# Row maxima inside the score contraction, narrower masks, the residual added on VectorE, and a leaner Q/K scratch

## The reference

```python
x = x + attn(layernorm(x), Wq, Wk, Wv, Wo)            # 16 heads of 16, 128 tokens
x = x + ssm(ctx, ctx, layernorm(x), ssm_kernel, D, 8) # 16 heads of 8, long convolution
x = x + ffn(layernorm(x), packed 4-bit weights, scales)

# attn: masked scores are ZERO, not minus infinity, before the softmax
scores = einsum('bthd,bshd->bhts', q, k) * tril(ones)
out = einsum('bhts,bshd->bthd', softmax(scores / 128 ** 0.5), v) @ Wo
# ssm: kv = k_i * v_j over time; y = causal convolution of kv with the head's kernel; out = (y + kv * D) . q
# ffn: (gelu_tanh(x Wg^T) * (x Wu^T)) Wd^T, MLP width 2048, each weight = 4-bit code * scale per block of 32
```

## Time and profile before

| | us |
|---|---|
| median of 3 runs (281.93 to 284.20) | 283.21 |
| profiled execution | 285.32 |
| its span in the profile | 283.6 |
| PE, DVE, ACT, POOL busy | 258.4, 160.6, 123.2, 157.2 |
| mean granted clock of TensorE | 0.973 |

### The profile page before, as it was taken

One profiled execution on the slowest core, in us unless ns is written; L12 is line 12 of the kernel. 1 busy time (PEld: TensorE's weight loads), 2 busy tenths in 40 slices (PEclk: granted clock), 3 DMA queues, 4 the chain that ended last, 5 costly groups with the idle time before them and its releaser, 6 DMA issues.

```text
span 283.6 us, 5339 instructions
## 1 busy us (share of the span) xinstructions
PE 258.4 (91%) x2056; PEld 167.5 (59%) x2056; DVE 160.6 (57%) x264; ACT 123.2 (43%) x257; POOL 157.2 (55%) x193
## 2 busy tenths in 40 slices
PE   0699999997999999996969999999999999999993
PEld 0355766555777777664634566666555666556662
DVE  2879633367775987897576584252635436131124
ACT  2354676553654545644426455323534253442240
POOL 3277264250514788799989897336445563723330
PEclk9999999997999999999579999999999999999998
DMA  6986969707120000003000200000303000000004
GB/s 208 380 296 198 225 203 225 160 4 218 37 82 0 2 2 2 1 3 111 2 0 1 83 30 0 2 0 0 113 0 103 11 0 2 1 0 2 0 0 149
DMA packets 16185, 20.27 MB, mean 71 GB/s; under 512 B 1056, under 2 KB 13856, under 8 KB 16160
## 3 DMA queue, kind: packets, MB, share of 16 engines
q1 hardware_dynamic: 16160, 19.93, 24.4%
HBM read 16.26 MB, written 3.67 MB: 70 GB/s over the span
## 4 chain that ended last, share of the span: by engine, by line
PE 67%; POOL 8%; DMA 7%; DVE 7%; SPq 4%; issue 3%; ACT 2%; DVEq 0%; ACTq 0%; POOLq 0%
PE bank L927 31%; PE bank L1097 14%; PE bank L1035 4%; DMA XN<-in_down_scale 4%; PE bank L999 3%; PE bank L1168 3%; PE bank L1055 3%; POOL w L473 3%; DMA qk_scratch<-pvs 2%; SPq L312 2%; POOL arena L457 2%; POOL arena L460 2%; DMA X<-in_x 1%; DVE arena L741 1%; PE bank L1158 1%
## 5 line engine op out<-in xcount | busy, mean ns | idle before, releaser
L481 POOL TENSOR_TENSOR QK<-QK 128x512 f16<-128x512 f32 x31 | 36.0, 1162 | 56.1 <-ACT QK L608 56.1
L848 DVE SCALAR_TENSOR_TENSOR QK<-bank,QK 128x512 f32<-128x512 f32 x32 | 22.1, 692 | 66.8 <-PE bank L927 66.8
L618 ACT ACTIVATE QK<-bank 128x512 f32<-128x512 f32 x32 | 19.1, 597 | 71.1 <-PE bank L927 71.1
L927 PE MATMUL bank<-xTh,Wa 128*128 128x512 f16 x128 | 40.9, 381 | 0.0
L927 PE MATMUL bank<-xTh,Wb 128*128 128x512 f16 x128 | 40.7, 379 | 0.0
L457 POOL TENSOR_TENSOR arena<-Ys,qx 128x640 f32<-128x640 f32 x16 | 25.1, 1570 | 8.8 <-ACT qx L660 8.8
L579 ACT ACTIVATE PT<-bank 128x1024 f32<-128x1024 f32 x16 | 16.4, 1023 | 27.4 <-PE bank L1039 27.4
L788 DVE TENSOR_REDUCE mx<-bank 128x8 f32<-128x1024 f32 x16 | 19.6, 1222 | 15.1 <-PE bank L1016 15.0
L927 PE MATMUL bank<-xTl,Wa 128*128 128x512 f16 x64 | 24.3, 380 | 0.0
L927 PE MATMUL bank<-xTl,Wb 128*128 128x512 f16 x64 | 24.3, 379 | 0.0
L1097 PE MATMUL bank<-Wa,QK 128*128 128x256 f16 x192 | 23.6, 273 | 0.0
(11 more groups left out here) (136 smaller groups left out, 522.1 us busy)
## 6 DMA issues: line engine op xcount, KB each, us to landing
QK<-qk_scratch SPq DMA_DIRECT2D x16, 256.0 KB, 6.0
arena<-in_codes SPq DMA_DIRECT2D x6, 384.0 KB
arena<-in_ker SPq DMA_DIRECT2D x2, 1024.0 KB, 12.5
qk_scratch<-Wa SPq DMA_DIRECT2D x16, 128.0 KB
arena<-in_ctx SPq DMA_DIRECT2D x2, 768.0 KB, 8.1
arena<-in_gu_scale SPq DMA_DIRECT2D x6, 256.0 KB
out<-XN SPq DMA_DIRECT2D x4, 256.0 KB, 2.4
Wb<-in_wqkv SPq DMA_DIRECT2D x3, 256.0 KB, 5.0
```

The lines of the kernel that those rows point to most:

```text
L481: g_.tensor_tensor(il[:, u % IR], val[:, u % VR], ih[:, u % IR], ALU.subtract).then_inc(s_il, 1)
L618: s_.activation(val[:, u % VR], bank[2 * (u % 2)][:, :], ACT.Gelu_apprx_tanh, scale=1.0 / W_GAIN).then_inc(s_gel, 1)
L848: v_.scalar_tensor_tensor(out=val[:, u % VR], in0=bank[2 * (u % 2) + 1][:, :], scalar=UP_SCALE, in1=val[:, u % VR], op0=ALU.mult, op1=ALU. ...
L927: ins = mmul(out, a(c), w(c), start=(n == 0), stop=(n == 3 * len(chunks) - 1))
```

## The change

- The row maxima, divided by `MAX_GAIN` = 8, are split into a high and a low fp16 part on DVE (`max_pieces`, three small operations; `guard_max` on POOL is gone). One fp16 product with an fp16 identity transposes the 32 columns, ACT copies them to `mT`, and SP copies them by DMA (`max_rows`, two for each batch) into rows 48, 49 and 112, 113 of `QK` on the Q side; the K side has -8 there, written once by four DMAs from `minus`. `scores_t` contracts 50 rows and has no products with `sel`; it waits for `s_rows`. `scores` contracts 48 rows.
- Q and K take 48 rows for a head instead of 64: scratch has two parts instead of three, laid out with the dimension of the head first (the columns of Wq and Wk are ordered for it), four stores fewer; eight of the sixteen loads have 16 rows instead of 32.
- `causal` has four products of 256 columns, with matrices (`nextb`, `prevb`, `above`, `below`) that say what the columns beyond the half need.
- RT is two fp32 transposes of R; DVE adds them to X, and ACT's copy is gone.
- `keep_busy` issues fp32 products of the identity whose results nobody reads: 18 before the first transposes of X, 4 before the second, 6 before the first projection.
- Orders and ticks: nine early heads of the convolution and one a tick after that (ten and two before), so ticks 0 to 6 hold one each; `DECODE` (1, 5, 18, 22) for (1, 5, 16, 22), `UNIT_TICKS` ends in 27, 28 for 28, 29. In a tick PE goes QT, scores, RT, MPT, convolve, YT, scores_t, TOK, OT, attend, PROJ, units. ACT goes ln_apply(2), the copy to `mT`, `em`, conv_out, OT, QT, probs, pv_out, ln_apply(1), units, w_hi_step, YT. DVE goes products, sum_slots(0), pair_max, sum_slots(1), w_lo, the addition of RT and its statistics, max_pieces, LN2, codes, normalise, YT, units. POOL goes decode_scale(1), conv_products(0), rstds(2), rstds(1), conv_products(1), decode_scale(0), products, act_lo.
- SP issues only codes 0 ahead of the rows of the maxima and codes 4 to 7 behind them; codes 1 to 3 are issued by ACT behind `w_hi_step` of the step before.

```diff
+    scr = nc.dram_tensor("qk_scratch", (2, 2, 2, DH, H, HALF), F16, kind="Internal").ap()
 
     ctx = ExitStack()
...
@@ -222,13 +228,14 @@
         (T_SCORES, T_SPLIT, T_MPT, T_ST, T_ATT, T_PVOUT, T_TOK, T_NORM, T_OT, T_PROJ, T_LN2, T_RSTD2, T_APPLY2,
          T_QT, T_MIX, T_MIX2, T_SUM, T_SUM2, T_RT, T_LN3, T_RSTD3, T_APPLY3, T_YT) = (
             0, 2, 3, 4, 5, 6, 7, 7, 8, 8, 8, 9, 9, 10, 11, 11, 12, 12, 13, 13, 14, 15, 15)
-        CONV_EARLY = 10
-        CONV_RATE = 2
-
-        UNIT_TICKS = (22, 23, 24, 24, 25, 26, 28, 29)
+        CONV_EARLY = 9
+        CONV_RATE = 1
+
+        UNIT_TICKS = (22, 23, 24, 24, 25, 26, 27, 28)
         EARLY = len(UNIT_TICKS) // 2
-        DECODE = (1, 5, 16, 22)
+        DECODE = (1, 5, 18, 22)
         DECODE_AHEAD = 7
+        WARM = (18, 4, 6)
 
 
...
@@ -303,47 +330,42 @@
                              bass.AP(ker_d.tensor, ker_d.offset + 1 + 8 * g * 384,
                                      [[1, P], [384, 8], [1, D]])).then_inc(s_toep[g], 16)
             sp.dma_start(wo[:, :, :], wo_d.rearrange("(c p) n -> p c n", p=P)).then_inc(s_w[3], 16)
+            sp.wait_ge(s_const, 3)
+            for g in range(2):
+                for par in range(2):
+                    sp.dma_start(QK[64 * par + 48:64 * par + 50, g, 1],
+                                 view(minus, [[0, H // 2], [1, HALF]])).then_inc(s_minus, 16)
             for g in range(2):
 
                 for k in range(2):
                     for m in range(2):
                         sp.wait_ge(s_qkl, 4 * g + 2 * k + m + 1)
-                        for part in range(3 if k == 0 else 2):
-                            sp.dma_start(scr[g, k, 8 * m:8 * m + 8, part],
-                                         nat[g][k][:, m, part % 2, :]).then_inc(s_scr[2 * g + k], 16)
+                        for part in range(2):
+                            sp.dma_start(scr[g, k, part, :, 8 * m:8 * m + 8],
+                                         nat[g][k][:, m, part, :]).then_inc(s_scr[2 * g + k], 16)
                 for k in range(2):
-                    sp.wait_ge(s_scr[2 * g + k], 96 if k == 0 else 64)
+                    sp.wait_ge(s_scr[2 * g + k], 64)
                     for par in range(2):
-                        for two in range(2):
-
-                            first = 1 if k == 0 and two else 0
-                            src = scr[g, k, par::2, first:first + 2].rearrange("h s d t -> (s d) h t")
-                            rows = 64 * par + 32 * two
-                            sp.dma_start(QK[rows:rows + 32, g, k, :, :],
+                        for first, parts, row in ((0, 2, 0), (0, 1, 32)) if k == 0 else ((0, 1, 0), (0, 2, 16)):
+                            src = scr[g, k, first:first + parts, :, par::2].rearrange("s d h t -> (s d) h t")
+                            rows = 64 * par + row
+                            sp.dma_start(QK[rows:rows + 16 * parts, g, k, :, :],
                                          src).then_inc(s_pack[g][k], 16)
...
-            for j in range(STEPS):
-                load_codes(j)
+            load_codes(sp, 0)
+
+            def max_rows(b):
+
+                sp.wait_ge(s_mt, b + 1)
+                for par in range(2):
+                    rows = 64 * par + 48
+                    sp.dma_start(QK[rows:rows + 2, b // 4, 0, :, P * (b % 4):P * (b % 4) + P],
+                                 mT[H * par:H * par + H, b % 2, :]).then_inc(s_rows[b % 2], 16)
+
+            for b in range(B):
...
@@ -782,12 +795,28 @@
             def pair_max(b, p):
 
                 n = 2 * b + p
-                if p == 0 and b >= 2:
-                    ve.wait_ge(s_mch, b - 1)
                 ve.wait_ge(s_s, n + 1)
                 v_.tensor_reduce(mx[:, b % 2, 8 * p:8 * p + 8],
                                  psum[:, 0:2, :].rearrange("p g (h t) -> p (g h) t", h=4),
                                  AX.X, ALU.max).then_inc(s_max, 1)
+
+            def max_pieces(b):
+
+                r = b % 2
+                ve.wait_ge(s_max, 2 * b + 2)
+                if b == 0:
+                    ve.wait_ge(s_const, 7)
+                if b >= 2:
+                    ve.wait_ge(s_em, b - 1)
+                    ve.wait_ge(s_mpt, b - 1)
+                hi = view(mp[:, r], [[16, 2], [4, 2], [1, 4]])
+                lo = view(mp[:, r], [[16, 2], [4, 2], [1, 4]], 8)
+                by_half = [[4, 2], [8, 2], [1, 4]]
+                v_.tensor_scalar(ms[:, r], mx[:, r], guard[:, 0:1], 1.0 / MAX_GAIN, ALU.max, ALU.mult).then_inc(s_ms, 1)
+                v_.tensor_scalar(hi, view(mx[:, r], by_half), guard[:, 0:1], 1.0 / MAX_GAIN,
+                                 ALU.max, ALU.mult).then_inc(s_ms, 1)
+                ve.wait_ge(s_ms, 2 * b + 2)
+                v_.tensor_tensor(lo, view(ms[:, r], by_half), hi, ALU.subtract).then_inc(s_mch, 1)
...
-                    pair_max(b, p)
-                for b in batch(t, T_LN3):
-                    ve.wait_ge(s_x2, b + 1)
-                    ln_stats(2, b)
                 for h in conv_heads(t + 1):
                     if h >= KVR:
                         products(h)
+                for b in batch(t, T_SUM):
+                    sum_slots(b, 0)
+                for b, p in pair_of_groups(t, T_SCORES):
+                    pair_max(b, p)
                 for b in batch(t, T_SUM2):
                     sum_slots(b, 1)
+                for j in early_decode(t, 3):
+                    w_lo(j)
+                for b in batch(t, T_LN3):
+                    ve.wait_ge(s_rt, b + 1)
+                    v_.tensor_tensor(X[:, b, :], X[:, b, :], bank[6][:, 0:D], ALU.add).then_inc(s_x2, 1)
+                    ve.wait_ge(s_x2, b + 1)
+                    ln_stats(2, b)
+                for b in batch(t, T_SPLIT):
...
@@ -907,9 +940,16 @@
             mmul = t_.matmul
             pe.wait_ge(s_const, 1)
 
+            def keep_busy(n):
+
+                for _ in range(n):
+                    mmul(bank[7][:, 0:P], ident[:, :], ident[:, :], start=True, stop=True)
+
             def transpose_x(g):
 
                 for pr in range(2 * g, 2 * g + 2):
+                    if g == 0:
+                        keep_busy(WARM[pr])
                     for b in (2 * pr, 2 * pr + 1):
...
@@ -953,6 +993,7 @@
                           lambda c: wqkvh[:, c, 2, :], lambda c: wqkvl[:, c, 2, :], range(2)).then_inc(s_v, 1)
 
             transpose_x(0)
+            keep_busy(WARM[2])
             project_qk(0)
             transpose_x(1)
             project_v(0)
...
@@ -987,18 +1028,21 @@
                 for lc in range(2):
                     convolve(h, lc)
 
-            def causal(banks, mask, swapped, full):
+            def causal(banks, transposed):
 
                 half = [slice(0, 64), slice(64, P)]
-                for k in (full, 1 - full):
-                    width = P if k == full else 64
-                    first = 64 if k == 1 and width == 64 else 0
+                for k in range(2):
                     for par in range(2):
                         rows = half[par]
-                        pick, m = (identb, mask) if par == k else (swapb, swapped)
-                        mmul(view(banks[par][:, :], [[P, 4], [1, width]], first), pick[rows, :],
-                             view(m[rows, first:first + width], [[0, 4], [1, width]]),
-                             start=(k == full), stop=False, skip_group_check=True)
+                        if transposed:
+                            pick = (identb if par else swapb) if k == 0 else prevb
+                            m, cut, first = (below, 1, 64) if k == 0 else (below, 0, 0)
+                        else:
+                            pick = (swapb if par else identb) if k == 0 else nextb
+                            m, cut, first = (above, 0, 0) if k == 0 else (above, 1, 64)
+                        mmul(view(banks[par][:, :], [[P, 4], [1, 64]], first), pick[rows, :],
+                             view(m[rows, cut:cut + 64], [[0, 4], [1, 64]]),
+                             start=(k == 0), stop=False, skip_group_check=True)
 
             def scores(b, p):
...
                     pe.wait_ge(s_max, n)
-                causal(bank[0:2], maskb, maskw, 0)
+                causal(bank[0:2], False)
                 for j in range(4):
                     for par in range(2):
                         pair = 4 * p + j
-                        rows = slice(64 * par, 64 * par + 64)
+                        rows = slice(64 * par, 64 * par + 48)
                         last = mmul(bank[par][:, P * j:P * j + P], QK[rows, b // 4, 0, pair, P * (b % 4):P * (b % 4) + P],
                                     QK[rows, b // 4, 1, pair, P * (b % 4):P * (b % 4) + P], start=False, stop=(j == 3),
...
@@ -1024,18 +1068,14 @@
                 if n == 0:
                     for lc in range(2):
                         pe.wait_ge(s_ys[lc], 2 * CONV_EARLY)
-                    pe.wait_ge(s_const, 7)
```

(45 more changed lines are left out.)

209 lines of the change are left out of this document (94 added, 115 removed).

## The result

The changed kernel takes 289.7 us (median, 288.9 to 290.3), against 282.6 of the kernel before on the same chip: ratio 1.024, 95% interval 1.020 to 1.028. It was forecast at 267.5, so the time is 22 us above the forecast and outside its range, and the sign is wrong.

What follows compares the result with a forecast made beforehand. PE was taken to bound the attention ticks and feed-forward part, POOL the stretch before the first unit. That unit 13.8 us sooner plus 1.9 behind it made 15.7 off the 283.21 median: 267.5 us, range 258 to 277.

Steps and rivals of the forecast that it cites:

- three small operations for the pieces of the maxima: DVE in ticks 10 to 17: three added operations per batch at 0.15 us each, bounds 0.3 and 0.9 together.
- Ticks 3 to 9: PE's leaner ticks with four moved convolutions: tick 8 starts at 70.7, 6.3 us ahead of 76.96.
- The period: Ticks 10 to 17: DVE becomes the bound, and the time per batch falls from 9.63 to 8.9 us only.
- The 24 us for batches 0 to 3: From `conv_products` of batch 0 to that of batch 3: 24 us instead of 27.70, reaching batch 3 at 104.9.
- The prices of PE: Savings per PE instruction read from the old trace: 25.1 us in all, with `scores_t` at about 0.55 us.
- A (the clock): Rival: PE, sparser in its ticks, falls to 1.2 GHz again and again; 275 us at half the time; chance 0.18.
- B (POOL keeps its pace): Rival: the 53.6 us from 88.95 to 142.59 stay, so the gain is some 10 us: 273; chance 0.14.
- C (PE the only bound): Rival: PE alone limits the kernel, so all 25 us come through: 258 us; chance 0.10.
- D (late rows of the maxima): Rival: the row transfer makes a 7.4 us path with PE's queue behind it each batch: 288 us; chance 0.05.
- to the first unit: Ticks 17 to 22: POOL's queue is the bound; the first unit starts at 134.7, 13.8 us sooner than 148.46.
- the X products: Behind the first unit's start: three of PE's removed products lay there, saving 3 x 0.64 = 1.9 us.

Runs made afterwards that it cites:

- e7: e1 plus three idle DVE operations per batch, SBUF to SBUF with results unread, ahead of the odd tick's pair maximum; 280.4 us.
- e8: e1 plus three idle DVE operations per batch, read from PSUM with results unread, ahead of the odd tick's pair maximum; 281.8 us.
- e10: e1 plus three idle DVE operations per batch, read from SBUF, at the old place of the pieces just ahead of L902; 291.2 us.
- e11: e1 plus three idle DVE operations per batch, read from PSUM, at the old place of the pieces just ahead of L902; 281.0 us.
- e9: The changed kernel with the pieces of the maxima still on DVE, moved to the odd tick behind the pair maximum; 282.4 us.
- e5: The changed kernel with the pieces of the maxima on POOL and the first two decodes at ticks 3 and 7; 276.1 us.
- e1: The changed kernel with the three small operations for the pieces of the maxima on POOL instead of DVE; 280.8 us.
- e2: The changed kernel with the first two decodes at ticks 3 and 7 instead of 1 and 5; 288.0 us.
- e3: The changed kernel with four idle PE products ahead of the mask of every `scores_t` and at the ends of ticks 17 to 21; 295.9 us.
- e13: e5 plus eight idle PE products at the end of each of ticks 17 to 21; 275.4 us.

## Why the prediction was wrong

**The step that failed: "three small operations for the pieces of the maxima (0.15 each ...; bounds 0.3 and 0.9 together)".** They took 14.2/8 = 1.8 us a batch, twice the upper bound. The price came from gaps and small rows of DVE; even with nothing to hold them the three take 0.62 together (0.22, 0.23 and 0.17). In this kernel an operation of DVE that reads and writes SBUF can be held until POOL's running operation ends (e7 against e8, e10 against e11). The old trace had signs of it: the decode of L813 took 0.56 us at one place and 0.53 to 1.27 in the six later ones, and L805, with two inputs in SBUF, took 0.42 to 1.24.
The Trainium skill (GPSIMD Engine Reference, Specifications and Key points) says that GpSimd shares its SBUF interfaces with VectorE and contends with VectorE instructions in a two-port mode or with two SBUF inputs. The trace agrees: `tensor_scalar` from SBUF and the two-input L819 are held, and the same `tensor_scalar` from PSUM isn't; in which mode it runs, no trace shows. The page gives no price; here it is up to 1.8 us for an operation of 0.16. It was a rule that spoke against the change, and the prediction did not weigh it.

**The place.** The prediction added the pieces to DVE's sum, as if only a full DVE could make them felt. They stood in DVE's queue ahead of L902; PE's next transpose of the maxima and `scores_t` wait for L902, and DVE's normalisation, with which its next round begins, waits for what PE does behind them. On such a loop what goes beyond its slack counts whether DVE is full or not. e10 against e11 shows it: 9.1 us more at this place cost 10.2, with DVE idle for 1.7 of 11.4 us. That the place alone decides is less sure, since in the odd tick (e7, e9) the operations were held for some 4 us only. Part of the cost goes by way of the clock: the granted clock is 0.918 in e10 and 0.951 in e11.

**"Ticks 3 to 9 ... Followed this puts the start of tick 8 at 70.7".** Batch 0 was forecast at 80.9 and came at 89.11. Codes landed at 52.16 (forecast 51.8) and the scores of tick 3 came at 56.37 (55.6), so the times up to there were right. One reading was not: the old PE did not stand still in ticks 2 and 3, its convolutions filled them, and the 6 us of standstill are new. Then the 8 us went. e5 has batch 0 at 79.99, so they are the pieces and the decode that stands in front of DVE's maxima together: alone, e1 wins 1.8 and e2 5.4 of it, both 9.1. That the convolutions moved behind a standstill of 6 us run at half of the clock, the prediction did not count.

**The period: 8.9 forecast, 28.73/3 = 9.6 up to batch 3, 10.9 from batch 3 to 4.** With the pieces away (e1) it is 25.13/3 = 8.4, under the forecast, with DVE busy for 23.40 and POOL for 23.48 us: the limits were the ones that it named, and the term for the pieces was wrong. The 24 us for batches 0 to 3 were also too few by the forecast's own terms: DVE's 22.50, three times 0.45 for the pieces and as much for the X additions make 25.2 of work, from which idle time can't be taken off.

**The prices of PE were right**: `scores_t` takes 0.55 us in tick 15 above (112.26 to 112.81), as forecast, and the two transposes of R 0.34 in e1 (105.07 to 105.41) against 0.24.

**Rivals.** A (the clock): the clock did fall, 0.62 at 56 to 66 us, 0.85 in the batches, 0.50 ahead of the first unit. Lifting it was worth little: e3 loses time by it, the idle products' own time included, and e13, which puts them where PE idles anyway, gets 0.7 us. How much of the loss beside the pieces the clock alone makes in the batches was not isolated. B (POOL keeps its pace): not in e1, where 55.8 us lie between batch 0 and the first unit against 59.5 before and 62.9 after. C (PE the only bound) fell: even e5 takes 276.1. D (late rows of the maxima) was the rival on the slower side, and it was not this: PE waited for them once, 1.6 us; the transfer took 3.32 at that place behind an issue of 0.60, and the whole path from ACT's copy 4.25 (76.05 to 80.30) against the 3.8 us of the forecast. The forecast had a chance of 0.04 for slower, and none of it for the mechanism that came.

**What is left.** e5 is 8.6 us above the forecast. Its own stages give: batch 0 0.9 sooner than forecast (79.99 against 80.9), batches 0 to 3 27.04 in place of 24, to the first unit 30.8 in place of 29.8, and behind it 136.3 in place of 133.2; that is 6.2, and 2.4 are between span and median, which the prediction had as 283.6 to 283.2 and which are 274.1 to 276.1 here. Windows of e5:

```profile
79.99:107.03 27.04, 22.13 (x282) 14.01 (x280) 23.60 (x40) 13.82 (x30) 24.51 (x37) 0.94 0.04 10
```

```profile
127.00:137.84 10.84, 5.99 (x17) 3.56 (x17) 9.02 (x14) 2.84 (x7) 10.30 (x12) 0.50 0.43 144
137.84:150.00 12.16, 11.69 (x53) 5.78 (x52) 8.63 (x16) 6.02 (x11) 11.40 (x12) 0.84 0.01 1
```

POOL is the busiest now, with 24.51 of the 27.04 us between batches 0 and 3; it has the pieces, about 3 us of it. Behind the first unit I had counted 1.9 us as saved, the X products. PE's busy time there is 129.7 us against 129.5 before, so nothing was. With the clock held (e13) it is 128.1 of 136.0 us, 1.4 less than before, but PE idles for 7.9 us against 5.6. So the clock took most of what the products gave, and waits would have taken it otherwise; which of the waits behind unit 0 sets the end was not tried.

## What to carry to other kernels

Before small operations are put into a queue, look at what stands behind them in it and whether that closes a loop between two engines; on a loop they cost what goes beyond its slack, with idle time on the engine or without. Price such an operation of VectorE from SBUF to SBUF by its longest row beside a working GpSimd, not by its shortest; it may be cheaper on GpSimd itself, or with PSUM as its source. And a lead won early is worth what the later stages can take: the same edit of the decodes gave 4.7, 1.8, 1.5 and -2.7 us in four versions of this kernel.

## What the runs showed of the hardware

- A `tensor_scalar` of 128x16 fp32 on VectorE took 0.14 to 1.79 us from SBUF and 0.14 to 0.18 from PSUM (24 of each, e7 and e8; SBUF destination in both). The long ones end with the end of a GpSimd operation; reductions with one input (L869: 1.20 to 1.22 us, 16 of them) and additions with one input in PSUM (L902: 0.41 to 0.42, 8 of them) kept their time beside GpSimd.
- Three such operations a batch at the wrong place cost 10.4 us of 281 (e10 against e1), and 0.2 with a PSUM source (e11).
- The small transfer from SBUF to SBUF for the rows of the maxima (16 rows of 256 bytes) took 3.3 us behind an issue of 0.6 on SyncE's queue.
